# Where the output weights' split parts are kept, and who splits them: projections two and three in place of one and two

## The chip, the cores and the metric
The kernel runs on 1 core of a Trainium2 chip. The metric is the device time of one execution in microseconds (us). A core has five engines that run their own instruction streams in order and meet only by semaphores: TensorE (PE; its weight loads are PEld), VectorE (DVE), ScalarE (ACT), GpSimd (POOL) and SyncE (SP), which here only issues DMAs.

## The reference, cut
Inputs are four sequences of 512 rows and 512 channels. Computed is x plus attention of a modulated x, and then that plus a feed-forward of it:

```python
x = x + _L0_attn_ref(_L0_cond_ref(x, f, f, cond_w, cond_u, cond_512), Wq, Wk, Wv, Wo, betas)
x = x + _L0_ffn_ref(_L0_cond2_ref(x, f, f, cond2_w, cond2_u, cond_512), W1, W2, W3)
```

The attention has 16 heads of 128 and segments of 128 rows: in each segment a masked softmax attention and a recall from a memory that is updated by a delta rule, both joined, and the joined heads multiplied by the output weights:

```python
att = beta * att_mem + (1.0 - beta) * att_dot
out = att.reshape(Bsz, SEG, H * DV) @ Wo
```

The modulation is a decaying scan over the rows in both directions, a division and a sigmoid. The feed-forward has 2048 hidden channels, a gate and a Hadamard transform.

## The kernel before, in words
Every large product is made of three matmuls of float32r operands: a value is split into a high part (a copy rounded to fp32r) and a low part (value less high part), and the products high x high, high x low and low x high are summed (lines 489 to 491). So each weight tile must be split before use.

The attention is a loop over n = 0..31: two heads of one of the four sequences in each step, eight steps for a sequence. In step n TensorE also computes v, k and q for step n + 1, between the pieces of the attention of step n. After each four steps, at n = 4, 8, ..., 28, comes a burst: `wo(m, dc)` for dc = 0..3 multiplies what the last four steps have gathered in ah/al by the output weights. It takes eight tiles, the parts o (8m + 2 dc + half), two for each dc. The eighth projection stands behind the loop. All eight projections use the same eight tiles again, so part m % 8 names the weights.

`STREAM` is the order in which weight tiles are used, and each takes the next of six ring slots (wh, wl: high and low, 512 KB each). A tile comes into its slot in one of two ways:
- split: SP loads two halves of 256 KB from the input into the four buffers called stage; ScalarE writes the high part (`split_hi`, line 1247; for v of later steps and q GpSimd does it), then GpSimd the low part (`split_w`, line 1623), or VectorE (`low_o`, line 952) where `by_vector` says so;
- fetched again: where `again` says so, SP fetches both parts, 1 MB, from HBM (lines 1802, 1803), where they were stored after an earlier split (`keep`, lines 1814, 1815; two stores of 512 KB) if `kept` says so.

Before the change, o parts 0 to 7 (the first projection, at n = 4) are split, low parts 4 to 7 by VectorE; at n = 8 the parts 8 to 11 are fetched and 12 to 15 split by ScalarE and GpSimd. Parts 0 to 3 are kept at n = 4 and parts 12 to 15 at n = 8. All later ones are fetched. The v, k and q tiles are split and kept for n < 8 and fetched from n = 8 on.

SP has one queue. In it the calls `keep(upto)` and `load_w(upto)` alternate, with arguments that count from `here`, the place of v of n + 1 in STREAM. `keep` waits until a tile is split; a stage load waits until the low part two tiles before has been made (it frees the buffer); a fetch waits until the slot's last user is done. While SP waits, all behind it waits. The modulation's work is laid between the attention's pieces in slots k = 0..7 of step n (`behind(n, k)`) by a planner, `shared_out`, that hands out scan, reciprocal and other steps by cost against a room for each slot. ROOM is for ordinary steps, BURST_ROOM for bursts, and FIRST_BURST_ROOM for n = 4 only. They differ in slots 4 and 5:

```python
BURST_ROOM = (700, 900, 2200, 4500, 3600, 4800, 2900, 4400)
FIRST_BURST_ROOM = (700, 900, 2200, 4500, 2200, 600, 2900, 4400)
```

VectorE's order in the second half of a step is: `behind(n, 4)`, low_o of the first part, `recalled(n, 2)`, `sums`, `join(n, 0)`, `add_wo(., 1)`, low_o of the second, `behind(n, 5)`, `join(n, 1)`, low_o of the third and fourth, `add_wo(., 2)`, `add_wo(., 3)`. TensorE's in a burst: wo 0, transposes and update, wo 1, recall and P times V (line 643), wo 2, wo 3, update, then k and q of n + 1. Each half of wo waits for its part (`wait_split`).

Of the kernel before, what the change touches and what calls it, by code (L numbers as in the profile page):

```python
# [84 lines left out]
def is_burst(n):  # L85
    return n % 4 == 0 and n > 0
# [73 lines left out]
PLACE = {x: i for i, x in enumerate(STREAM)}  # L160
# [21 lines left out]
def kept(i):  # L182


    kind, m = STREAM[i]
    return kind in "vkq" and m < 8 or kind == "o" and (m < 4 or 12 <= m < 16)


def again(i):

    kind, m = STREAM[i]
    return kind in "vkq" and m >= 8 or kind == "o" and m >= 8 and not kept(i)


def by_scalar(i):
# [4 lines left out]
def by_vector(i):  # L200

    kind, m = STREAM[i]
    return kind == "o" and 4 <= m < 8


SPLIT = [i for i in range(NW) if not again(i)]
# [18 lines left out]
def adaln_attn_ffn(nc, xT_d, fT_d, cond_d, wu_d, wq_d, wk_d, wv_d, wo_d, betas_d,  # L225
# [9 lines left out]
    with ExitStack() as ctx:  # L235
# [170 lines left out]
        def halves(i, half):  # L406

            s = stage[(2 * SPLIT_NO[i] + half) % NSTAGE]
            hi, lo = ring(i)
            if STREAM[i][0] == "2":  # L410
                return (hi[:, :].rearrange("p (a n d) -> p n a d", a=2, n=8)[:, 4 * half:4 * half + 4],
                        lo[:, :].rearrange("p (a n d) -> p n a d", a=2, n=8)[:, 4 * half:4 * half + 4],
                        s[:, :].rearrange("p (n a d) -> p n a d", n=4, a=2))
            return hi[:, 512 * half:512 * half + 512], lo[:, 512 * half:512 * half + 512], s[:, :]
# [385 lines left out]
        def vector(e):  # L800
# [112 lines left out]
            def behind(n, k):  # L913
                for name, i, _ in STEPS[at[0]:UPTO[n, k]]:
                    if name[:2] == "lv":
                        level(i, int(name[2]))
                    elif name == "lo":
                        low_w2(i)
                    elif name in ("t0", "t1", "t2", "t3"):
                        z_times(i, int(name[1]))  # L920
                    elif name in ("nf", "nb", "df", "db", "mn", "mu", "ni", "n2", "di", "d2", "d3", "rc0", "rc1",
                                  "rc2", "rc3", "oy"):
                        scan(i, name)
                at[0] = UPTO[n, k]
# [21 lines left out]
            def low_o(m):  # L946

                i = PLACE["o", m]
                for half in range(2):
                    hi, lo, raw = halves(i, half)  # L950
                    w.wait_ge(a_wh, HI_A[i] + half + 1)
                    e.tensor_tensor(lo, raw, hi, ALU.subtract).then_inc(v_wl, 1)

            def maxima(n, j):
                w.wait_ge(d_mk, 16)
                w.wait_ge(d_b[0], 16)
                w.wait_ge(d_b[1], 16)
                w.wait_ge(pe_s, 2 * n + j + 1)
                w.wait_ge(pe_pt, 2 * (n - 1) + j + 1)
                w.wait_ge(a_p, 2 * (n - 1) + j + 1)  # L960
                for s in range(NSEG):
                    m = e.tensor_tensor_reduce(S[:, j, seg(s)], X[j][:, seg(s)], mask[:, :], 1.0, NEG, ALU.add,  # L962
                                               ALU.max, st[:, 0, j, s:s + 1])
                m.then_inc(v_mr, 1)
                w.wait_ge(v_mr, 2 * n + j + 1)
                e.tensor_scalar(st[:, 1, j, :], st[:, 0, j, :], -SCALE, None, ALU.mult).then_inc(v_mx, 1)
# [53 lines left out]
            def sigma(n, kind, j):  # L1020
                src, dst = (kT, sk) if kind == "k" else (qT, sq)
                w.wait_ge(a_kc if kind == "k" else a_qc, 2 * n + j + 1)
                w.wait_ge(a_ke if kind == "k" else a_qe, 2 * n + j + 1)
                if kind == "k":
                    w.wait_ge(pe_am, 6 * (n - 1) + 2 + j + 1)
                else:
                    w.wait_ge(pe_am, 6 * (n - 1) + 4 + j + 1)
                e.scalar_tensor_tensor(dst[:, j, :], src[:, j, :], 1.0, etmp[j][:, :], ALU.add,
                                       ALU.max).then_inc(v_sk if kind == "k" else v_sq, 1)
# [105 lines left out]
            for n in range(NN):  # L1135
                nx = n + 1
                more = nx < NN
                maxima(n, 0)
                maxima(n, 1)
                sigma(n, "q", 0)  # L1140
                behind(n, 0)
                if n > 0:
                    low_att(n - 1)
                sigma(n, "q", 1)
                behind(n, 1)
                memory(n, 0)
                if not more:
                    gate(0, 0, "1", G[0])
                behind(n, 2)
                recalled(n, 1)  # L1150
                if not more:
                    gate(0, 0, "3", G[1])
                behind(n, 3)
                memory(n, 1)
                if is_burst(n):
                    add_wo(n // 4 - 1, 0)
                behind(n, 4)
                if n == 4:
                    low_o(4)
                recalled(n, 2)  # L1160
                sums(n)
                join(n, 0)
                if is_burst(n):
                    add_wo(n // 4 - 1, 1)
                if n == 4:
                    low_o(5)
                if not more:
                    gate(0, 1, "1", G[0])
                if more and not is_burst(n):
                    sigma(nx, "k", 0)  # L1170
                behind(n, 5)
                join(n, 1)
                if n == 4:
                    low_o(6)
                    low_o(7)
                if is_burst(n):
                    add_wo(n // 4 - 1, 2)
                    add_wo(n // 4 - 1, 3)
                memory(n, 2)
                join(n, 2)  # L1180
                behind(n, 6)
                recalled(n, 3)
                join(n, 3)
                if is_burst(n):
                    sigma(nx, "k", 0)
                if more:
                    sigma(nx, "k", 1)
                else:
                    gate(0, 1, "3", G[1])
                behind(n, 7)  # L1190
# [572 lines left out]
        def sync(e):  # L1763
# [24 lines left out]
            def load_w(upto):  # L1788

                while load[0] < min(upto, NW):  # L1790
                    i = load[0]
                    load[0] += 1
                    if not again(i):
                        load_half(i, 0)
                        load_half(i, 1)
                        continue
                    kind, m = STREAM[i]
                    first = PLACE[kind, m % 8 + (8 if kind == "o" and m % 8 >= 4 else 0)]
                    w.wait_ge(d_keep[SLOT[first]], 32 * saves(SLOT[first], first + 1))
                    wait_used(w, BEFORE[i])  # L1800
                    hi, lo = ring(i)
                    e.dma_start(hi[:, :].bitcast(F32), high_s[kind][m % 8]).then_inc(d_back[SLOT[i]], 16)
                    e.dma_start(lo[:, :].bitcast(F32), low_s[kind][m % 8]).then_inc(d_back[SLOT[i]], 16)
# [63 lines left out]
            for n in range(NN):  # L1867
                nx, burst = n + 1, is_burst(n)
                more = nx < NN
                here = PLACE["v", nx] if more else PLACE["1", 0]  # L1870
                behind(n, 0)
                keep(here + 2)
                load_w(here + (6 if burst and n > 4 else 4))
                behind(n, 1)
                if n > 2 and is_burst(n - 2) and (n - 2) // 4 % 2 == 0:
                    fetch_x((n - 2) // 8)
                behind(n, 2)
                keep(here + 3)
                load_w(here + (8 if burst and n > 4 else 5))
                behind(n, 3)  # L1880
                if burst:
                    keep(here + 4)
                    load_w(here + (10 if n > 4 else 7))
                behind(n, 4)
                keep(here + (6 if burst else 4))
                load_w(here + (10 if burst else 6))
                behind(n, 5)
                if burst:
                    keep(here + 9)
                    load_w(here + 12)  # L1890
                behind(n, 6)
                if burst:
                    keep(here + 11)
                    load_w(here + 14)
                if more:
                    keep(here + (13 if burst else 5))
                    load_w(here + (15 if burst else 7))
                behind(n, 7)
# [104 lines left out]
```

## Time and profile before

| | us |
|---|---|
| median of 3 runs | 1669.19 |
| lowest and highest | 1668.13, 1670.24 |
| the profiled execution | 1668.93 |
| its span, first to last instruction | 1667.0 |
| TensorE busy | 1573.6 (94%) |
| VectorE busy | 1159.5 (70%) |
| ScalarE busy | 744.5 (45%) |
| GpSimd busy | 563.0 (34%) |
| moved by DMA | 264.39 MB |
| granted TensorE clock, mean | 0.989 |

The views are of the profiled execution; its times count from the first instruction, so 1.9 us of the 1668.93 lie around the span. An engine's idle time matters only where TensorE has to wait for it in the end. A granted clock of 1.00 is 2.4 GHz and 0.50 is 1.2 GHz.

### The profile page before, as it was taken

The page shows a single profiled execution, that of the slowest core. Times are in us where ns is not written, and L with a number is a line of the kernel's source. Part 1 is how long each engine was busy: PE and PEld are TensorE (multiplying, and loading weights), DVE is VectorE, ACT ScalarE, POOL GpSimd, SP SyncE. Part 2 cuts the span into 40 slices and gives each one's busy share as a digit, 9 for nine tenths or more (in the row PEclk, how much of TensorE's full clock was granted, in tenths as well). Part 3 has the DMA queues.
Part 4 walks back from the last instruction along what each step waited for, and adds up shares of the span by engine and source line. Part 5 has one row for each costly group of instructions (what it writes and reads, how often), then busy time and mean ns, then how long its engine had stood idle before and what let it go on. Part 6 is the DMA issues. An engine that isn't in the chain of part 4 may idle for free.

```text
span 1667.0 us, 26932 instructions
## 1 busy us (share of the span) xinstructions
PE 1573.6 (94%) x9696; PEld 1406.6 (84%) x9696; DVE 1159.5 (70%) x2688; ACT 744.5 (45%) x1623; POOL 563.0 (34%) x406
## 2 busy tenths in 40 slices
PE   0689979999999999999999999998999999999999
PEld 0579969898998999899999899888788888888887
DVE  8788959887888887887765763665787885333333
ACT  3366636535535534643554562652544442222221
POOL 4476555241232122121102100133655463343331
PEclk9799999999999999999999999999999999999999
DMA  3466566458365367456447646447211222221101
GB/s 135 153 212 209 189 239 236 174 185 334 136 228 196 125 230 253 146 187 224 162 157 283 233 179 240 142 153 252 90 57 51 65 68 105 98 64 39 51 14 51
DMA packets 111491, 264.39 MB, mean 159 GB/s; under 512 B 11088, under 2 KB 36096, under 8 KB 110464
## 3 DMA queue, kind: packets, MB, share of 16 engines
q1 hardware_dynamic: 92784, 235.41, 39.6%
q10 hardware_dynamic: 18576, 27.27, 5.3%
q8 instruction: 78, 1.28, 0.3%
q14 instruction: 53, 0.43, 0.1%
HBM read 214.38 MB, written 48.25 MB: 158 GB/s over the span
## 4 chain that ended last, share of the span: by engine, by line
PE 84%; DVE 8%; issue 3%; DMA 2%; ACT 1%; POOL 1%; ACTq 0%; SPq 0%; DVEq 0%; POOLq 0%
PE psG L489 15%; PE psG L491 15%; PE psG L490 15%; PE psX L489 3%; PE psX L643 3%; PE psX L490 3%; PE psX L491 3%; PE psX L598 3%; PE psZ L624 3%; PE psZ L615 2%; PE psZ L623 2%; PE psZ L490 2%; PE psZ L491 2%; PE psY L490 2%; PE psZ L489 2%
## 5 line engine op out<-in xcount | busy, mean ns | idle before, releaser
L1623 POOL TENSOR_TENSOR wl<-stage,wh 128x512 fp32r<-128x512 f32 x160 | 227.7, 1447 | 170.0 <-ACT wh L1247 168.7
L489 PE MATMUL psG<-yh,wh 128*128 128x512 f32 x632 | 258.2, 409 | 9.9 <-ACT etmp L1388 7.5
L491 PE MATMUL psG<-yh,wl 128*128 128x512 f32 x632 | 247.7, 392 | 0.0
L490 PE MATMUL psG<-yl,wh 128*128 128x512 f32 x632 | 247.4, 391 | 0.0
L1686 POOL TENSOR_TENSOR vs<-v,omb 128x512 f32<-128x512 f32 x64 | 95.9, 1519 | 340.7 <-PE psX L643 333.7
L1693 POOL TENSOR_TENSOR hl<-sg,hh 128x512 fp32r<-128x512 f32 x64 | 86.5, 1351 | 227.6 <-ACT hh L1462 227.5
L489 PE MATMUL psG<-ah,wh 128*128 128x256 f32 x512 | 146.7, 287 | 2.8 <-POOL wl L1623 1.7
L489 PE MATMUL psG<-wh,yh 128*128 128x256 f32 x496 | 146.8, 296 | 0.0
L489 PEld LDWEIGHTS psG<-yh,wh 128*128 128x128 f32 x632 | 119.9, 190 | 31.0 <-issue 8.1
L491 PE MATMUL psG<-ah,wl 128*128 128x256 f32 x512 | 144.9, 283 | 0.0
L490 PE MATMUL psG<-al,wh 128*128 128x256 f32 x512 | 144.8, 283 | 0.0
L491 PEld LDWEIGHTS psG<-yh,wl 128*128 128x128 f32 x632 | 119.2, 189 | 25.8
L491 PE MATMUL psG<-wh,yl 128*128 128x256 f32 x496 | 140.5, 283 | 0.0
L490 PE MATMUL psG<-wl,yh 128*128 128x256 f32 x496 | 140.4, 283 | 0.0
L490 PEld LDWEIGHTS psG<-yl,wh 128*128 128x128 f32 x632 | 120.0, 190 | 20.0
L1247 ACT ACTIVATE wh<-stage 128x512 fp32r<-128x512 f32 x154 | 89.1, 622 | 104.9 <-PE psZ L491 30.6
L1462 ACT ACTIVATE hh<-sg 128x512 fp32r<-128x512 f32 x64 | 40.5, 632 | 173.1 <-DVE sg L1048 173.1
L881 DVE RECIPROCAL DBK<-DF 128x128 f32<-128x128 f32 x120 | 107.8, 927 | 0.6
L1380 ACT ACTIVATE kT<-psG 128x512 f32<-128x512 f32 x62 | 37.0, 596 | 157.6 <-PE psG L491 157.6
L1413 ACT ACTIVATE S<-S,st 128x128 f32<-128x128 f32 x256 | 99.2, 389 | 17.1 <-issue 14.0
L489 PE MATMUL psX<-yh,wh 128*128 128x512 f32 x128 | 52.0, 407 | 56.4 <-POOL wl L1623 47.6
L962 DVE CUSTOM_DVE_ANT_0 S<-psX,mask 128x128 f32<-128x128 f32 x256 | 59.4, 286 | 65.7 <-PE psX L598 65.4
(197 smaller groups left out, 4267.6 us busy)
## 6 DMA issues: line engine op xcount, KB each, us to landing
wh<-high_o SPq DMA_DIRECT2D x52, 512.0 KB, 3.9
wl<-low_o SPq DMA_DIRECT2D x52, 512.0 KB, 5.2
stage<-in_w SPq DMA_DIRECT2D x64, 256.0 KB, 3.9
wh<-high_v SPq DMA_DIRECT2D x24, 512.0 KB, 4.0
wl<-low_v SPq DMA_DIRECT2D x24, 512.0 KB, 5.4
wh<-high_k SPq DMA_DIRECT2D x24, 512.0 KB, 4.2
wl<-low_k SPq DMA_DIRECT2D x24, 512.0 KB, 5.8
wh<-high_q SPq DMA_DIRECT2D x24, 512.0 KB, 4.5
```

What stands on the lines that cost most here:

```text
L489: e.matmul(out, lh, rh, start=first, stop=False, skip_group_check=check)
L490: e.matmul(out, lh, rl, start=False, stop=False, skip_group_check=check)
L491: return e.matmul(out, ll, rh, start=False, stop=last, skip_group_check=check)
L598: m = e.matmul(X[j][:, seg(s)], qT[:, j, seg(s)], kT[:, j, seg(s)], start=True, stop=True)
L624: e.matmul(Z[j][:, 129:258], sq[:, j, seg(s)], mem[:, j, 0:P + 1], start=True, stop=True).then_inc(pe_am, 1)
L881: e.reciprocal(dbk[:, 128 * j:128 * j + 128], df[:, 128 * j:128 * j + 128]).then_inc(v_rc, 1)
L962: m = e.tensor_tensor_reduce(S[:, j, seg(s)], X[j][:, seg(s)], mask[:, :], 1.0, NEG, ALU.add, ALU.max, st[:, 0, j, s:s + 1])
L1247: e.activation(hi, raw, ACT.Copy).then_inc(a_wh, 1)
L1413: m = e.activation(S[:, j, seg(s)], S[:, j, seg(s)], ACT.Exp, bias=st[:, 1, j, s:s + 1], scale=SCALE, accum_out=st[:, 2, j, s:s + 1])
L1623: e.tensor_tensor(lo, raw, hi, ALU.subtract).then_inc(p_wl, 1)
L1686: e.tensor_tensor(vs[:, :, j, :], v[n % 2][:, :, j, 0:P], omb[:, 128 * j:128 * j + 128].rearrange("p (a d) -> p a d", a=1).to_broadcast([P ...
L1693: e.tensor_tensor(hl[u % 2][:, j, :], hid(k)[:, :], hh[u % 2][:, j, :], ALU.subtract).then_inc(p_hl, 1)
```

## The change
The o parts kept are now 8 to 11 (at n = 8) and 20 to 23 (at n = 12), none at n = 4. Fetched are m >= 16 of parts 0 to 3 and m >= 24 of parts 4 to 7. So at n = 4 eight parts are split and none kept; at n = 8 eight parts are split, 12 to 15 with VectorE making the low parts, and 8 to 11 kept; at n = 12 parts 16 to 19 are fetched, and 20 to 23 split by ScalarE and GpSimd and kept. Over the kernel eight parts more are split and eight fewer fetched; eight are kept as before. SP's load arguments that held for n = 4 now hold for n = 8 too. The planner's rooms are left as they are.

```diff
     kind, m = STREAM[i]
-    return kind in "vkq" and m < 8 or kind == "o" and (m < 4 or 12 <= m < 16)
+    return kind in "vkq" and m < 8 or kind == "o" and (8 <= m < 12 or 20 <= m < 24)
...
-    return kind in "vkq" and m >= 8 or kind == "o" and m >= 8 and not kept(i)
+    return kind in "vkq" and m >= 8 or kind == "o" and m >= (16 if m % 8 < 4 else 24)
...
-    return kind == "o" and 4 <= m < 8
+    return kind == "o" and m < 16 and m % 8 >= 4
...
                 behind(n, 4)
-                if n == 4:
-                    low_o(4)
+                if n in (4, 8):
+                    low_o(2 * n - 4)
                 recalled(n, 2)
                 sums(n)
                 join(n, 0)
                 if is_burst(n):
                     add_wo(n // 4 - 1, 1)
-                if n == 4:
-                    low_o(5)
+                if n in (4, 8):
+                    low_o(2 * n - 3)
...
                 behind(n, 5)
                 join(n, 1)
-                if n == 4:
-                    low_o(6)
-                    low_o(7)
+                if n in (4, 8):
+                    low_o(2 * n - 2)
+                    low_o(2 * n - 1)
...
-                    first = PLACE[kind, m % 8 + (8 if kind == "o" and m % 8 >= 4 else 0)]
+                    first = PLACE[kind, m % 8 + ((8 if m % 8 < 4 else 16) if kind == "o" else 0)]
...
-                load_w(here + (6 if burst and n > 4 else 4))
+                load_w(here + (6 if burst and n > 8 else 4))
...
-                load_w(here + (8 if burst and n > 4 else 5))
+                load_w(here + (8 if burst and n > 8 else 5))
...
-                    load_w(here + (10 if n > 4 else 7))
+                    load_w(here + (10 if n > 8 else 7))
```

## Rows read from the trace of the kernel before

**Rows 1.** The page, part 1: busy us, share of the span, instructions.
```profile
PE 1573.6 (94%) x9696; PEld 1406.6 (84%) x9696; DVE 1159.5 (70%) x2688; ACT 744.5 (45%) x1623; POOL 563.0 (34%) x406
```

**Rows 2.** TensorE's waits, 100 to 420 us: total, times, longest.
```profile
PE psG L489 <- ACT etmp L1388: 7.5, 1, 7.5
PE psG L489 <- DMA wl<-low_q: 2.4, 1, 2.4
PE psG L489 <- POOL wl L1623: 1.7, 1, 1.7
PE psG L489 <- DVE wl L952: 1.0, 1, 1.0
```

**Rows 3.** The chain that ended last, n = 4: start, length, what.
```profile
221.45 3.01 DVE wl L952 x2
...
227.76 4.11 DMA stage<-in_wk
...
237.05 1.61 POOL wl L1623
...
239.57 5.75 DMA stage<-in_wk
...
247.75 0.77 PE psG L489
```

**Rows 4.** SP's queue in order of time, n = 4: start, length, what.
```profile
208.12 7.08 SPq L1786 DMA_DIRECT2D stage<-in_wo  x4
...
216.24 8.62 SPq L1786 DMA_DIRECT2D stage<-in_wo  x4
```

**Rows 5.** VectorE in order of time, n = 4: its subtractions of weights.
```profile
221.36 3.09 DVE L952 TENSOR_TENSOR wl<-stage,wh 128x512 fp32r<-128x512 f32 x2
...
226.41 2.48 DVE L952 TENSOR_TENSOR wl<-stage,wh 128x512 fp32r<-128x512 f32 x4
```

**Rows 6.** VectorE in order of time, n = 8: start, length, operation, [idle before].
```profile
343.99 1.22 DVE L835 TENSOR_TENSOR_SCAN DF<-dec,EK 128x512 f32<-128x512 f32 x1
...
356.12 1.76 DVE L881 RECIPROCAL DBK<-DF 128x128 f32<-128x128 f32 x2
358.72 0.17 DVE L984 RECIPROCAL rz<-psZ 128x2 f32<-128x2 f32 x1 [0.83 <-PE psZ L624]
...
361.22 0.41 DVE L1037 TENSOR_TENSOR xb<-xb,psG 128x256 f32<-128x256 f32 x1
361.55 1.76 DVE L881 RECIPROCAL DBK<-DF 128x128 f32<-128x128 f32 x2
...
364.19 2.12 DVE L835 TENSOR_TENSOR_SCAN DF<-dec,EK 128x512 f32<-128x512 f32 x1
...
368.41 0.58 DVE L1010 SCALAR_TENSOR_TENSOR pT<-psX,st,t 128x128 f32<-128x128 f32 x2
```

**Rows 7.** TensorE in order of time, n = 8: quarter's start, update behind, stalled q.
```profile
360.67 0.36 PE L489 MATMUL psG<-ah,wh 128*128 128x256 f32 x1
...
372.26 0.61 PE L615 MATMUL psZ<-delta,kn 128*128 128x129 f32 x4
...
381.18 0.50 PE L489 MATMUL psG<-yh,wh 128*128 128x512 f32 x1 [2.37 <-DMA wl<-low_q]
```

**Rows 8.** SP's queue in order of time, n = 8.
```profile
364.12 0.32 SPq L1830 DMA_DIRECT2D ratio_s<-OY  x1
...
371.95 1.13 SPq L1802 DMA_DIRECT2D wh<-high_q  x1
```

**Rows 9.** TensorE by microsecond: stretch, us, busy, granted clock, DMA share, GB/s.
```profile
244.00:245.00 1.00, 0.00 (x0) 0.60 0.92 238
...
251.00:252.00 1.00, 1.00 (x6) 0.99 1.07 369
```

**Rows 10.** Stretch: PE, PEld, DVE, ACT, POOL busy; granted clock, DMA share, GB/s.
```profile
225.00:235.00 10.00, 9.87 (x79) 9.57 (x78) 5.36 (x13) 3.40 (x6) 3.54 (x4) 1.00 0.50 159
```

**Rows 11.** SP's queue in order of time, n = 12.
```profile
489.99 0.32 SPq L1802 DMA_DIRECT2D wh<-high_q  x1
```

## The prediction, made before the changed kernel was run

> **What bounds the kernel now.** The page comes first: TensorE is busy 94% of the span [rows 1], so a change can win only where TensorE stands still, and loses wherever it makes TensorE wait. Second, who waited for whom on TensorE between 100 and 420 us, the stretch that holds the first two output projections (n = 4 and n = 8): it stood 7.5 us for ScalarE's etmp, 2.4 us for the low part of a q weight, 1.7 us and 1.0 us for the low parts of output weights [rows 2]. The 7.5 and the 1.7 and 1.0 lie at n = 4, the 2.4 at n = 8. So the two bursts hold 12.6 us that could be won. Third, the chain that ended last through the 7.5 us [rows 3]. Fourth, the queues in order of time on SP, VectorE and TensorE, for n = 4 [rows 4, 5] and n = 8 [rows 6 to 8].
>
> **n = 4, what the change takes away.** Four keeps go (parts 0 to 3: eight stores of 512 KB, 4.2 MB). SP passes straight on to its stage loads: the loads that start at 208.12 no longer stand behind the keep of part 2, and those at 216.24 no longer behind the keep of part 3 [rows 4], a gain of 1 to 3 us for when parts 4 and 6 land. Is that on the path? The chain says no [rows 3]. What ends the 7.5 us is: VectorE splits part 5 (221.45), later parts 6 and 7; that frees the stage into which k of n = 5 is loaded (227.76, 4.1 us to land); GpSimd splits k and then q (until 238.7); SP, which keeps q first, then loads k of n = 6 (239.57, 5.75 us to land); ScalarE, which has that split ahead of etmp in its order, gets there at 247. VectorE's start on part 5 follows its join(n, 0), which waits for TensorE's own P times V, not for a part 4 or 5 that came late. All keeps left in that chain are those of k, q and v, and they stay. The stores of part 3, issued by 216, are over long before 227: from 225 to 235 the DMA engines are busy 0.50 [rows 10]. So I price the removal at nothing, cover being this chain. Bounds: a gain of all of it, 7.5 us of standing plus what the clock gives back (below), if the landings of 4.1 and 5.75 us are short of bandwidth because of older stores; and nothing on the other side, since no wait is added at n = 4.
>
> A page of the Trainium skill, "DMA: Bandwidth & Descriptors" (section "Where 436 GB/s comes from"), puts the ceiling of a core's ports at about 435 GB/s; by it the 4.2 MB are an estimated 9.6 us of transfer, and if the burst were bound by transfer the change would win about that. The share of 0.50 ahead of the chain's first landing speaks against it here.
>
> **n = 8, first what goes.** Parts 8 to 11 are no longer fetched (4 x 1 MB) but loaded (4 x 0.5 MB) and split; the same number of keeps stands there, but of parts 8 to 11, which come before and early in the burst as those of parts 0 to 3 did at n = 4. Now the keeps of 12 to 15 are held up by the store of OY to ratio_s at 364.12, go out in a bunch, and push the fetch of q to 371.95 [rows 8]; it lands late and TensorE stands 2.37 us at 381.18 [rows 7]. Afterwards no keep follows that store, q is fetched right behind it, around 368 to 369, and TensorE asks for it later. I take the whole 2.4 us as won.
>
> **n = 8, what comes.** VectorE gets the low parts of 12 to 15: eight subtractions. Four in a row took 2.48, so 0.62 each, but the two of part 5, beside GpSimd's multiplication of V, took 3.09 together [rows 5]. Where they stand in VectorE's order matters more than their 5 us: parts 14 and 15 stand behind behind(8, 5) and join(8, 1). At n = 4 the plan leaves only a short step there (FIRST_BURST_ROOM has 600 in place of 4800), and this plan is not changed for n = 8. So at n = 8 two reciprocals, OY and two scans stand ahead of part 14. Working it out in before's times:
> 1. VectorE ends its two reciprocals at 357.88 and has 0.83 us free before the recall [rows 6]. Part 12 takes 1.24, ends 359.1: everything up to the add at 361.22 comes 0.4 later.
> 2. GpSimd now splits parts 10 and 11 from 345 to 354, beside VectorE's scans, which slows both: a scan took 2.12 beside GpSimd and 1.22 without it [rows 6]. Bounds 0 to 1.1 us; I take 0.35. So part 13 starts at 361.55 + 0.75 = 362.3.
> 3. Part 13 is, as part 5 was, beside the multiplication of V: 3.09, ends 365.4 (bounds 1.24 and 3.09).
> 4. Two reciprocals and OY: 364.19 - 361.55 = 2.64, to 368.0 [rows 6].
> 5. Two scans: 368.41 - 364.19 = 4.2 us before, with GpSimd splitting beside them [rows 6]. That splitting is gone, so I take twice 1.15 (1.22 less the overlap of neighbours), 2.3, to 370.3; bounds 2.3 and 4.2.
> 6. join(8, 1) 0.5, then part 14, 1.24: 372.0.
>
> TensorE: the third quarter of the projection starts at 360.67, and two quarters end at 372.26, so a quarter is 5.8 and a part 2.9 [rows 7]. It wants part 13 at 363.57 and gets it at 365.4: 1.85 us. It would start the last quarter at 360.67 + 5.8 + 1.85 = 368.3 and gets part 14 at 372.0: 3.7 us. Part 15 is ready 1.24 later, in time. Sum 5.55. Behind the stall stand the k and q projections of n = 9 on TensorE; VectorE waits for them, so it recovers there, and its order behind part 15 was idle for 3 us before.
>
> ScalarE's eight copies and GpSimd's four pairs for 8 to 11 come as at n = 4, ahead of need; but two are close. Part 11 is due about 355 (ahead of 360.67 by a part, 2.9, and the recall and P times V), and ScalarE takes it after an exponential that waits for VectorE until about 350, so GpSimd ends it near 354. And ScalarE copies part 12 before it copies pT, which TensorE needs for P times V near 359, and part 12 lands, as part 4 did, some 5 us after its load was issued, near 356. Both priced at 0, bound 1 us each.
>
> **n = 12.** It becomes the old n = 8: four fetched, four split by ScalarE and GpSimd and kept. There the keeps cost 2.37 us through the store to ratio_s. At n = 12 the tiles are of the first modulation, whose OY isn't stored, so nothing bunches them. The fetch of q, at 489.99 now [rows 11], would wait until part 23 is kept, about 498, and is wanted at 510. Priced at 0, bound 2.4.
>
> **Sum.** -2.4 + 5.55 = +3.2 on a profiled execution of 1668.93 us (span 1667.0), which is 0.26 below the median of the three, 1669.19 (1668.13 to 1670.24). 1669.19 + 3.2 = 1672.4; from the profiled one 1672.1. Between them I say 1672.3.
> Bounds of this case: step 3 at its low end and step 2 at 0 give part 14 at 369.9, a stall of 3.4, and +1.0: 1670. Every step at its upper end: part 14 at about 375.5, a stall of 9, and +6.7: 1676.
>
> **Rivals.**
> 1. The forecast, VectorE late with 13 and 14, clock kept: 1672.3. Chance 0.34.
> 2. The same with the clock lost. At n = 4 TensorE stood until 247.75 for 7.5 us [rows 2, 3], from 240.2, and in the microsecond from 244 the granted clock was 0.60, on its way from 2.4 to 1.2 GHz; it was back only from 251 (0.99), though work began at 247.75 [rows 9]. So about 3.3 us of work went at half speed: 1.6 us more. A stall of 3.7 us, with one of 1.85 three us before it, comes near the four microseconds after which it fell there. 1672.3 + 1.7 = 1674.0. Chance 0.22. (The Trainium skill, "TensorE: Matmul & The Clock Gate", section "What's actually happening", has a throttled default that activity releases; the rows above agree.)
> 3. The other side: the old stores do hold up the landings at n = 4, and the 7.5 us go with 1.6 of clock. Against it: the chain [rows 3] and the 0.50 [rows 10]. For it: 5.75 us to land where others took less. 1672.3 - 9.1 = 1663.2, less where only part of it goes. Chance 0.12.
> 4. VectorE's new work finds room (the steps ahead of part 14 run faster, or part 13 does), and the q stall goes: between -2.4 and +0.5, about 1667.3. Against it: VectorE's order there [rows 6], which leaves no gap of this size between 361.2 and 368.4. Chance 0.16.
> 5. More is late: part 11 or pT, scans slowed after all, or the 2.4 us return at n = 12. From one of these at full size, with the clock: 1677. Chance 0.16.
>
> **How the numbers follow.** A measurement can tell about 0.2%, 3.3 us, from no change: 1665.9 and 1672.5 are the borders. Faster: rival 3 and a little of 4, 0.14. The same: most of 4 (0.14) and two thirds of 1 (0.22), 0.36. Slower: the rest of 1 (0.12), 2 and 5, 0.50. The range leaves out rival 3 and the tail of 5: 1666 to 1677. The case of my forecast alone spans 1670 to 1676.
>
> **What would show it.** In the profile after: TensorE waits for VectorE's wl at n = 8 in two places, 1 to 2 us and 3 to 4 us; scans of VectorE stand between its first and second pair of subtractions there; no wait for low_q; the 7.5 us for etmp at n = 4 unchanged within 1 us; no new wait at n = 12; GpSimd's wl count up from 160 to 168, VectorE's from 8 to 16, ScalarE's wh by 16; 4.2 MB less moved. The prediction is wrong if the etmp wait shrinks, or if VectorE's part 14 is done by 368.

## The result
The changed kernel takes 1675.74 us (median of 6 runs, 1673.14 to 1678.43), the kernel before 1669.53 beside it (6 runs, 1668.13 to 1670.45). The ratio is 1.0038, 95% interval 1.0025 to 1.0051: 6.3 us slower, 4.2 to 8.5. Run again beside two of the experiments it was 1677.16 against 1671.70, ratio 1.0032, 1.0021 to 1.0042. The forecast was 1672.3 with a range of 1666 to 1677, and slower by over 0.2% had a chance of 0.50. The profiled execution took 1675.9, its span is 1673.9 against 1667.0.

The page after, to set beside [rows 1], and the line of the bytes moved:

```profile
PE 1578.8 (94%) x9696; PEld 1411.1 (84%) x9696; DVE 1169.0 (70%) x2696; ACT 754.0 (45%) x1639; POOL 572.8 (34%) x414
...
DMA packets 111492, 260.21 MB, mean 155 GB/s; under 512 B 11088, under 2 KB 36096, under 8 KB 110464
```

Counts and bytes are as announced: 8 instructions more on VectorE and GpSimd each, 16 on ScalarE, 4.2 MB less moved. TensorE does the same 9696 matmuls and is busy 5 us longer, in part since some of them ran at the lower clock (below).

TensorE's waits after, from 100 to 420 us, to set beside [rows 2] (waiting instruction, what it waited for: total, times, longest):

```profile
PE psG L489 <- ACT etmp L1388: 6.3, 1, 6.3
PE psG L489 <- DVE wl L952: 5.7, 3, 3.5
PE psG L489 <- POOL wl L1623: 1.9, 2, 1.7
```

and from 420 to 700 us, where the kernel before had no wait for a weight:

```profile
PE psG L489 <- DMA wl<-low_q: 2.0, 1, 2.0
```

Three things are to be seen: etmp's wait at n = 4 is 1.2 us shorter, VectorE's low parts cost 4.7 us more, and the wait for low_q has moved from the first to the second stretch.

To see where the 6.9 us of span came from I took the last step of each quarter of a projection, VectorE's add into xb (line 1037), as a mark. From the two traces in order of time:

| stretch | before | after | difference |
|---|---|---|---|
| start to first add at n = 4 | 211.87 | 212.89 | +1.02 |
| n = 4, first to last add | 21.99 | 22.00 | 0.01 |
| to the first add at n = 8 | 118.87 | 118.51 | -0.36 |
| n = 8, first to last add | 19.73 | 26.39 | +6.66 |
| to the first add at n = 12 | 112.00 | 109.11 | -2.89 |
| n = 12, first to last add | 19.73 | 19.74 | +0.01 |
| to the first add at n = 16 | 109.52 | 110.86 | +1.34 |
| to the last add of the last projection | 534.54 | 534.39 | -0.15 |
| to the end of the span | 518.75 | 520.01 | +1.26 |

The first and the last line are not the change's: in the profiles of all kernels of this study the first add lies between 210.9 and 212.9, and the last stretch between 517.3 and 520.4, with no order in them; the changed kernel itself, run again, has 517.75 us in the last stretch where it had 520.01. What lies between sums to +4.6 (+4.8 in the changed kernel run again).

VectorE after, in order of time, through n = 8, to set beside [rows 6]:

```profile
357.68 1.76 DVE L881 RECIPROCAL DBK<-DF 128x128 f32<-128x128 f32 x2
359.36 1.92 DVE L952 TENSOR_TENSOR wl<-stage,wh 128x512 fp32r<-128x512 f32 x2
...
363.26 0.41 DVE L1037 TENSOR_TENSOR xb<-xb,psG 128x256 f32<-128x256 f32 x1
363.59 2.16 DVE L952 TENSOR_TENSOR wl<-stage,wh 128x512 fp32r<-128x512 f32 x2
365.67 1.75 DVE L881 RECIPROCAL DBK<-DF 128x128 f32<-128x128 f32 x2
367.46 0.75 DVE L886 SCALAR_TENSOR_TENSOR OY<-NF,tf,DBK 128x512 f32<-128x512 f32 x1
368.32 1.22 DVE L835 TENSOR_TENSOR_SCAN DF<-dec,EK 128x512 f32<-128x512 f32 x1
369.46 1.20 DVE L838 TENSOR_TENSOR_SCAN NF<-dec,EKV 128x512 f32<-128x512 f32 x1
370.57 0.58 DVE L1010 SCALAR_TENSOR_TENSOR pT<-psX,st,t 128x128 f32<-128x128 f32 x2
371.07 2.49 DVE L952 TENSOR_TENSOR wl<-stage,wh 128x512 fp32r<-128x512 f32 x4
```

The two scans stand ahead of parts 14 and 15 (the last row, four subtractions), and VectorE has no gap. TensorE in order of time, to set beside [rows 7]:

```profile
361.62 0.36 PE L489 MATMUL psG<-ah,wh 128*128 128x256 f32 x1
...
365.90 0.36 PE L489 MATMUL psG<-ah,wh 128*128 128x256 f32 x1 [1.16 <-DVE wl L952]
...
372.51 0.55 PE L489 MATMUL psG<-ah,wh 128*128 128x256 f32 x1 [3.50 <-DVE wl L952]
```

It waits 1.16 us for part 13 and 3.50 for part 14. And TensorE by microsecond (stretch, us, busy, granted clock, DMA share, GB/s):

```profile
371.00:372.00 1.00, 0.00 (x0) 0.98 1.00 281
372.00:373.00 1.00, 0.49 (x2) 0.50 0.71 229
...
375.00:376.00 1.00, 1.00 (x9) 0.81 1.05 428
```

The clock fell to 1.2 GHz at the end of the 3.5 us, just before part 14 was ready, and was back within 375: 2.9 us of work at half speed, 1.4 us lost. Of the 6.66 us at n = 8 the two waits are 4.7, the clock 1.4, and 0.2 is a wait for GpSimd's part 11; 0.4 is not assigned.

### The profile page after: what moved, and what is told of

Its sections match the earlier page's. It is cut to its first block, busy times and chain, and to the rows that moved or that the text cites. A ratio compares the mean times of both kernels' runs of the same rounds, so it can differ in the third digit from the quotient of the medians.

```text
span 1673.9 us, 27003 instructions
## 1 busy us (share of the span) xinstructions
PE 1578.8 (94%) x9696; PEld 1411.1 (84%) x9696; DVE 1169.0 (70%) x2696; ACT 754.0 (45%) x1639; POOL 572.8 (34%) x414
## 4 chain that ended last, share of the span: by engine, by line
PE 83%; DVE 9%; issue 3%; DMA 2%; ACT 1%; POOL 1%; ACTq 0%; SPq 0%; DVEq 0%; POOLq 0%
PE psG L489 15%; PE psG L491 15%; PE psG L490 15%; PE psX L489 3%; PE psX L490 3%; PE psX L491 3%; PE psX L643 3%; PE psX L598 3%; PE psZ L624 2%; PE psZ L615 2%; PE psZ L623 2%; PE psY L490 2%; PE psY L489 2%; PE psZ L490 2%; PE psZ L491 2%
## 5 line engine op out<-in xcount | busy, mean ns | idle before, releaser
L1623 POOL TENSOR_TENSOR wl<-stage,wh 128x512 fp32r<-128x512 f32 x168 | 242.1, 1466 | 184.5 <-ACT wh L1247 183.2
L1247 ACT ACTIVATE wh<-stage 128x512 fp32r<-128x512 f32 x170 | 98.8, 622 | 114.3 <-PE psZ L491 31.4
L489 PEld LDWEIGHTS psG<-ah,wh 128*128 128x128 f32 x512 | 98.7, 193 | 8.8 <-issue 7.4
```

The source lines that it names most:

```text
L489: e.matmul(out, lh, rh, start=first, stop=False, skip_group_check=check)
L1247: e.activation(hi, raw, ACT.Copy).then_inc(a_wh, 1)
L1623: e.tensor_tensor(lo, raw, hi, ALU.subtract).then_inc(p_wl, 1)
```

## The experiments
All ratios are against the kernel before on the same chip, with 95% intervals. The kernel before had medians of 1669.5 to 1672.2 in the comparisons, as much as most effects here, so I go by the ratio and by the stretches between adds.

### VectorE's help alone
On the kernel before, with `low_o` of 2n - 4 to 2n - 1 called at n = 8 too:
```diff
-    return kind == "o" and 4 <= m < 8
+    return kind == "o" and m < 16 and m % 8 >= 4
...
-                if n == 4:
+                if n in (4, 8):
...
```

> The kernel before with the other part of the change alone: VectorE makes the low parts of 12 to 15 at n = 8 in place of GpSimd; every keep and fetch lies as before. Theory (VectorE's order is what costs): TensorE waits for VectorE's wl at n = 8, 4 to 6 us in all, with a clock fall of 1 to 2 us more; the keeps of 14 and 15 come later and push the fetch of q, so its wait stays. Time 4 to 8 us over before, as much as the whole change or more. Rival (GpSimd's extra four parts are what made the difference): within 2 us of before.

1675.23 us, ratio 1.0022 (1.0012 to 1.0032), 3.7 us slower (2.0 to 5.4); the profiled execution has a span of 1673.9, as the whole change. TensorE's waits from 340 to 400 us, first of this kernel:

```profile
PE psG L489 <- DVE wl L952: 4.5, 2, 3.5
PE psG L489 <- DMA wl<-low_q: 1.2, 1, 1.2
```

and of the changed kernel:

```profile
PE psG L489 <- DVE wl L952: 4.7, 2, 3.5
PE psG L489 <- POOL wl L1623: 0.2, 1, 0.2
```

The same 3.5 us. From first to last add at n = 8 it takes 27.3 us. So VectorE's part alone makes a loss of this size; by the ratio its middle is a little under the 4 to 8 that I gave it. The clock cost more here than in the changed kernel: it was back only in 378, so work from 372.30 on lost some 3 us, against 1.4.

### The keeps moved, without VectorE
On the changed kernel, with the condition put back in all three places:
```diff
-    return kind == "o" and m < 16 and m % 8 >= 4
+    return kind == "o" and 4 <= m < 8
...
-                if n in (4, 8):
+                if n == 4:
...
```

> The changed kernel with the low parts of 12 to 15 left to GpSimd, as before the change; the keeps lie as in the changed kernel. Theory: TensorE has no wait for VectorE's wl at n = 8, at most 2 us for GpSimd's; no q wait at n = 8 (saved 2.4), a q wait of about 2 us at n = 12: in all 1668 to 1671, the same as before. Rival (moving the keeps is itself what costs): 1674 or more though VectorE splits nothing at n = 8.

1669.55 us, ratio 0.9992 (0.9981 to 1.0004): no difference from before. At n = 8 there are 21.2 us from first to last add, 1.4 over before, of which 1.1 are waits for GpSimd's wl; the wait for low_q is 2.1 us and lies at n = 12. The rival, that moving the keeps is what costs, falls.

### One half of the keeps, without VectorE
On the kernel before:
```diff
-    return kind in "vkq" and m < 8 or kind == "o" and (m < 4 or 12 <= m < 16)
+    return kind in "vkq" and m < 8 or kind == "o" and (m < 4 or 20 <= m < 24)
...
-    return kind in "vkq" and m >= 8 or kind == "o" and m >= 8 and not kept(i)
+    return kind in "vkq" and m >= 8 or kind == "o" and (8 <= m < 12 or m >= 16) and not kept(i)
```

> The kernel before with one half of the change, without VectorE's help: parts 0 to 3 are kept at n = 4 as before; the keeps of the other half move from 12 to 15 (n = 8) to 20 to 23 (n = 12), split by GpSimd. Theory (the four keeps and the split carry their own q stall with them): the wait for low_q at n = 8 goes, one of about 2 us comes at n = 12, time as before within 2 us. Rival (n = 12 has room, as I forecast): no q wait at all and 2 to 3 us faster.

1668.77 us, ratio 0.9988 (0.9977 to 0.9999). Its only wait for low_q is 1.8 us, at n = 12; the stretch from n = 8 to 12 is 109.1 (2.9 shorter), that from 12 to 16 110.9 (1.4 longer). The stall goes where the keeps go. This is the place where the rival was my own forecast, that n = 12 has room, and by the wait it fell. The time is less clear: 2.0 us faster by the ratio (0.2 to 3.8) lies on the border between the two expectations, and in the profile the stall costs 1.4 us at n = 12 where it had cost 2.9 at n = 8.

### No stores at n = 4
The kernel before without the keeps of parts 0 to 3. It leaves out their stores and later fetches v tiles of the same size in their place, so it computes the projections from the second on with wrong weights and serves for timing alone:
```diff
-    return kind in "vkq" and m < 8 or kind == "o" and (m < 4 or 12 <= m < 16)
+    return kind in "vkq" and m < 8 or kind == "o" and 12 <= m < 16
...
+                    if kind == "o" and m % 8 < 4:
+                        kind = "v"
...
```

> The kernel before without the keeps of parts 0 to 3 (eight stores of 512 KB at n = 4), and later fetches of those parts read the kept v tiles of the same size in their place, so the projections from the second on are computed with wrong weights; all else is equal. Theory (the chain of splits sets the 7.5 us at n = 4, the stores do not): etmp's wait stays between 6 and 8 us, time 1668 to 1670.5. Rival (the stores hold up the landings): the wait falls by 3 us or more and time to 1666 or less.

1671.16 us, ratio 1.0009 (0.9999 to 1.0019). etmp's wait is 6.3 us, as in the changed kernel, 7.5 before. The stretch from the last add at n = 4 to the first at n = 8 is 118.2. Over the profiles it lies between 118.2 and 119.2 in the three kernels that store at n = 4 and keep SP's order there (mean 118.7), and between 117.1 and 118.5 in the seven that don't store (mean 118.0). So the four keeps at n = 4 are worth some 0.7 us in that stretch, from ranges that overlap, and rival 3, which gave them 7.5 us and the clock, falls. The total is no evidence here, since this kernel's q stall at n = 8 was longer: 4.0 us and a clock fall, 3.9 us more than before in the stretch to n = 12. SP's queue and TensorE there:

```profile
368.25 0.70 SPq L1804 DMA_DIRECT2D wh<-high_q  x1
```
```profile
381.68 0.80 PE L489 MATMUL psG<-yh,wh 128*128 128x512 f32 x1 [4.01 <-DMA wl<-low_q]
```

Here q's fetch was issued 3.7 us earlier than in the kernel before (371.95, [rows 8]), and TensorE waited 1.6 us longer for it. The time of issue alone doesn't set this stall.

### SP's order at n = 4
On the kernel before:
```diff
+                if n == 4:
+                    load_w(here + 13)
                 if burst:
                     keep(here + 11)
                     load_w(here + 14)
```

> The kernel before with one change in SP's order at n = 4: the stage loads of k of n = 6 go ahead of the keeps of k and q of n = 5. Theory (those loads stand behind the keep of q and land behind its 1 MB): they are issued at about 236 and 238.5 in place of 239.6, land by 242, etmp's wait falls from 7.5 to 3 to 5 us, and time by 3 to 5 us, to about 1665. Rival (ScalarE's or GpSimd's own work is next late, or the keeps only trade places): under 1 us gained.

1666.41 us, ratio 0.9975 (0.9963 to 0.9988), 4.2 us faster. etmp's wait is 3.4 us. SP's queue and ScalarE in this kernel, in order of time:

```profile
235.03 3.05 SPq L1786 DMA_DIRECT2D stage<-in_wk  x2
238.12 0.43 SPq L1814 DMA_DIRECT2D high_k<-wh  x1
```
```profile
237.62 0.64 ACT L1247 ACTIVATE wh<-stage 128x512 fp32r<-128x512 f32 x1 [1.26 <-DMA stage<-in_wk]
240.90 0.63 ACT L1247 ACTIVATE wh<-stage 128x512 fp32r<-128x512 f32 x1 [2.64 <-DMA stage<-in_wk]
```

Both halves of k are there by 240.9, where the chain of [rows 3] had them at 245.3. That the chain runs through the keep of q, as the prediction read it, is shown. The loads also landed faster: ScalarE had the first half 2.6 us after its issue (235.03 to 237.62), where behind the keep of q it took 5.75 us to land [rows 3].

### SP's order at n = 4 and n = 8
The edit above, and on the kernel before:
```diff
+                if n == 8:
+                    load_w(here + 11)
                 if burst:
                     keep(here + 9)
                     load_w(here + 12)
```

> The kernel before with two changes in SP's order: at n = 4 k of n = 6 is loaded ahead of the keeps of k and q of n = 5, and at n = 8 q of n = 9 is fetched ahead of the keeps of parts 13 to 15. Theory: the gain of the first alone (4 to 5 us) plus the q wait at n = 8 (2.2 us): 6 to 7 us faster than before. Rival (the keeps are pushed onto v, k, q of the next steps and stall there): no more than the first alone.

1660.83 us, ratio 0.9948 (0.9936 to 0.9961): 8.7 us faster, the best kernel of the study. No wait for low_q is left, etmp's is 3.3 us. Between first add and last it takes 929.05 us, 7.3 less than before, a little over the 6 to 7 expected; the rest of the span's 8.3 is in the two outer stretches that vary anyway.

### The changed keeps with that order
On the changed kernel: GpSimd in place of VectorE, `load_w(here + 13)` ahead at n = 4 and `load_w(here + 11)` ahead at n = 12.

> The changed keeps and splits, with GpSimd in place of VectorE for 12 to 15, and SP's order altered as in the fastest kernel so far: at n = 4 k of n = 6 is loaded ahead of the keeps of k and q, at n = 12 q of n = 13 is fetched ahead of the keeps of 21 to 23. Theory (what the change moves is worth nothing by itself once the q stall is gone at either place): no wait for low_q, etmp's wait 2 to 4 us, time within 3 us of that fastest kernel, 0.993 to 0.996 of before. Rival (having no stores at n = 4 is worth something with the loads ahead): 2 us or more under it.

1663.79 us, ratio 0.9953 (0.9941 to 0.9965), no wait for low_q, etmp's 2.9. The stretch from n = 12 to 16 is 109.53 us, as long as before (109.52), where the kernel with the keeps moved, which differs there in SP's order alone, has 111.18: the order of q's fetch and the keeps makes the stall at n = 12. The intervals of this and the last kernel overlap, from two comparisons. By the stretches splitting 8 to 11 in place of fetching them costs 1.3 us at n = 8 (21.0 us from first to last add, of which 1.0 are waits for GpSimd's wl), and elsewhere I see no worth in where the keeps lie once SP's order is mended.

### The plan's rooms
On the changed kernel:
```diff
+SECOND_BURST_ROOM = (700, 900, 2200, 4500, 2200, 600, 2900, 10000)
...
-        left = min(left, 0) + (FIRST_BURST_ROOM if n == 4 else BURST_ROOM if is_burst(n) else ROOM)[k]
+        left = min(left, 0) + (FIRST_BURST_ROOM if n == 4 else SECOND_BURST_ROOM if n == 8 else BURST_ROOM if is_burst(n) else ROOM)[k]
```

> The changed kernel with the planner's rooms at n = 8 cut in slots 4 and 5 as at n = 4 (2200 and 600 in place of 3600 and 4800), the steps taken out laid into slot 7 (10000 in place of 4400), so that the plan is the same again at n = 9. Theory (VectorE's order sets the loss at n = 8): the wait for part 14 (3.5 us before a clock fall) is gone or under 0.7 us, the clock stays up at n = 8, part 13 may still cost 1 to 2 us, and time falls by 3.5 to 6 us against the changed kernel, to about 1670 to 1672. Rival (GpSimd's and ScalarE's extra splitting sets the loss, or the moved steps come late elsewhere): time stays within 1.5 us of the changed kernel's 1675.7, with waits of the same sum in n = 8 or n = 9.

1678.27 us, ratio 1.0054 (1.0036 to 1.0072). The stall for part 14 went: 21.2 us from first to last add at n = 8. But the rival had it right: TensorE stood again, 5.8 us, at the scores of n = 9. TensorE's wait from 370 to 400, and ScalarE in order of time:

```profile
PE psX L599 <- issue: 5.8, 1, 5.8
```
```profile
390.41 0.72 ACT L1260 ACTIVATE EU<-EU,wu 128x512 f32<-128x512 f32 x1 [3.35 <-DVE EU L823]
391.04 0.58 ACT L1381 ACTIVATE qT<-psG 128x512 f32<-128x512 f32 x1
```

The trace gives no releaser for that wait, but the copy of q to qT, which the scores need, stands in ScalarE's order behind two exponentials that wait for VectorE's moved steps, and the scores start at 391.72. The reading is from order and times; the next run bears it out.

The same with 4400 in slot 7 and the 5600 spread over n = 9, 700 in each slot:

> The changed kernel with the rooms at n = 8 cut in slots 4 and 5 as at n = 4, and the 5600 taken out spread over the eight slots of n = 9, 700 each (the earlier try had them all in slot 7 of n = 8, where ScalarE waited for VectorE ahead of the copy of q and TensorE stood 5.8 us). Theory: the waits for parts 13 and 14 stay as small as in that try (about 1 us), the 5.8 us at the scores of n = 9 go, and time is 1669 to 1672 against 1675.7 of the changed kernel. Rival (VectorE is full around n = 9 wherever the steps lie): a wait of 3 us or more appears in n = 9 or 10.

1671.60 us, ratio 1.0001 (0.9992 to 1.0011). The 5.8 us are gone, VectorE's wl cost 2.0 us over n = 4 and n = 8 together, and q at n = 12 3.0.

### VectorE's order
The changed kernel once more, and then with `low_o(2 * n - 2)` and `low_o(2 * n - 1)` of n = 8 ahead of `behind(n, 5)` and `join(n, 1)`:
```diff
+                if n == 8:
+                    low_o(2 * n - 2)
+                    low_o(2 * n - 1)
                 behind(n, 5)
                 join(n, 1)
-                if n in (4, 8):
+                if n == 4:
```

> The changed kernel once more, on the same chip as the next two, for comparison: 3 to 8 us over before; waits for VectorE's wl at n = 8 of 1.2 and 3.5 us, for low_q at n = 12 of 1 to 3 us.

> The changed kernel with one thing altered: at n = 8 VectorE makes the low parts 14 and 15 ahead of behind(8, 5) and join(8, 1), not behind them. Plan, keeps and fetches stay. Theory (the place in VectorE's order costs, not its amount of work): from the first to the last add of the projection at n = 8 some 21.5 us in place of 26.4, the wait for part 14 under 0.5 us, no fall of the clock there, time 4 to 6 us under the changed kernel and so within 2 us of before. Rival (VectorE has too much to do around n = 8 wherever it stands): the stall reappears behind the burst, and less than 2 us is gained.

1677.16 (1.0032, 1.0021 to 1.0042) against 1670.17 (0.9999, 0.9989 to 1.0010): the same work in another order is 5.5 us faster by the ratios. The changed kernel run again has the waits expected: 1.16 and 3.50 us for VectorE's wl at n = 8 and 2.3 for low_q at n = 12. VectorE in the kernel with its order altered, in order of time:

```profile
361.63 3.32 DVE L952 TENSOR_TENSOR wl<-stage,wh 128x512 fp32r<-128x512 f32 x4
366.52 1.29 DVE L952 TENSOR_TENSOR wl<-stage,wh 128x512 fp32r<-128x512 f32 x2 [1.56 <-ACT wh L1250]
```

Part 14 is done at 364.95, TensorE doesn't wait for it, and part 15 waits only for its high part. The wait for part 13 is still 1.16 us. The stretch at n = 8 is 22.4 us (26.4 in the changed kernel, run again), 0.9 over the 21.5 expected, part of it since the last two adds now wait for VectorE. No stall came back behind the burst.

## Why the prediction was right, and where it was off
**n = 4, the stores priced at nothing.** Held in the main, not to the letter. From the last add there to the next burst it is -0.36 us in the pair of profiles, 0.7 in the mean of ten. But the prediction called itself wrong if etmp's wait shrank, with a margin of 1 us, and it shrank by 1.2 (7.5 to 6.3), by 1.6 in the changed kernel run again (5.9). The kernels with the stores at n = 4 and SP's old order have 6.1 to 7.6 us, the seven without the stores 5.5 to 6.3, so a small part of the wait did stand on the stores. Most of the 1.2 was lost again in the clock. It came back at 251 before [rows 9], but only within 252 in the changed kernel:

```profile
251.00:252.00 1.00, 1.00 (x4) 0.50 1.07 332
252.00:253.00 1.00, 1.00 (x5) 0.75 0.93 281
```

So 5.0 us of work from 247.53 on went at half speed where 3.3 had, 0.9 us more lost. The rest of rival 3 is answered by two runs: without the stores nothing like 7.5 us is gained, with the loads ahead of the keeps 4.2 us are. By the Trainium skill's ceiling of about 435 GB/s in "DMA: Bandwidth & Descriptors" ("Where 436 GB/s comes from") the same 4.2 MB would have been an estimated 9.6 us. No gain of that size shows here, since the chain waits on an order and not on those bytes.

**n = 8, VectorE late.** Held in its order and nearly in its sum. Counted from the first add at n = 8, which came 0.67 later than before, part 14 was done at 371.07 + 1.24 - 0.67 = 371.6 in before's times; the sum had 372.0. The terms inside were off and nearly cancelled. VectorE ended its reciprocals 0.9 us later rather than 0.35, most of it in one step that took 1.51 us beside GpSimd's EKV where it had taken 0.41:

```profile
356.13 1.51 DVE L877 TENSOR_SCALAR DF<-DF 128x512 f32<-128x512 f32 x1
```

Part 12 took 1.92 beside another multiplication, 0.7 over its 1.24; the steps up to the add gave 0.4 back, and part 13 started at 362.9 in place of 362.3. It took 2.16, not 3.09. The two scans took 2.25, as forecast (2.3); but GpSimd's splitting had stood beside the first of them only, until 365.2, and two other multiplications of GpSimd beside the rest. The two stalls were 1.16 and 3.50 where 1.85 and 3.7 were forecast, 4.7 in place of 5.55. That the place of parts 14 and 15 in VectorE's order is the cause of the second is shown by two kernels that leave its work as it is and change its order or its plan.

**The clock.** The case with it had 0.22, that without it 0.34; it came, 1.4 us where I had put 1.7. At n = 8 it fell in all three profiles that have the wait of 3.50 us, and cost 1.4, 1.5 and, with VectorE's help alone, some 3 us. At n = 4 it went either way. TensorE's clock in the kernel with SP's order mended there, after a wait of 3.4 us for etmp:

```profile
242.00:243.00 1.00, 0.35 (x2) 0.99 1.02 418
243.00:244.00 1.00, 1.00 (x4) 0.50 1.04 426
```

and in the one with both orders mended, after 3.3 us:

```profile
243.00:244.00 1.00, 0.00 (x0) 1.00 1.04 426
244.00:245.00 1.00, 0.89 (x4) 1.00 1.00 410
```

The one fell to 1.2 GHz, the other did not. No run here shows what decides between them, so that the size of 1.7 was nearly met is in part luck.

**The q stall at n = 8.** Held: -2.89 in its stretch, 2.4 forecast; q's fetch was issued at 368.66, 368.0 in before's times, where 368 to 369 was forecast.

**n = 12 priced at nothing.** This step failed. The forecast looked only at the store to ratio_s, which bunches the keeps at n = 8, and put the fetch of q at 498 in before's times. It was issued then: 502.38, and this burst lay 4.44 later. But SP in order of time shows what stands ahead of it:

```profile
495.37 0.42 SPq L1802 DMA_DIRECT2D wh<-high_k  x1
...
496.31 0.43 SPq L1814 DMA_DIRECT2D high_o<-wh  x1
...
501.50 0.84 SPq L1815 DMA_DIRECT2D low_o<-wl  x1
502.38 0.80 SPq L1802 DMA_DIRECT2D wh<-high_q  x1
```

The keeps of all four parts are bunched here too, behind the stage loads, the last of which waits for part 21 (done at 494.9) and was issued by 495.3. TensorE wants q at 514.98 and gets it only at 516.95, 13.7 us after the issue of its low part at 503.23. I had counted when the fetch is issued, and not what the engines had still to move: from 500 to 525 they were busy 0.99 to 1.03 in each stretch of 5 us, at 398 to 415 GB/s. What was issued before q is not the whole of it. By the GB/s of those stretches I estimate that the 6.6 MB issued from 495 up to and with q would have been moved by about 513, in time; but 8.0 MB were moved from 495 to 517, so the fetches of v and k issued behind it, at 505 and 508, took a share. That is argued from these numbers; that SP's order makes the stall is shown by the run with q's fetch ahead of the keeps. The term is +1.34 in place of 0.

**Sum.** Forecast -2.4 + 5.55 = +3.2. Measured between the marks: -0.36 + 6.66 - 2.89 + 1.34 - 0.13 = +4.6, and 6.3 (4.2 to 8.5) by the runs, 5.4 (3.5 to 7.0) the second time. In the pair of profiles the other 2.3 us of the span lie in the two stretches that vary from profile to profile; why the medians differ by more than 4.6 is not settled. What came is not the case called most likely, with its clock kept (1672.3, chance 0.34), but rival 2 together with the stall at n = 12 that rival 5 names (0.16). The clock and n = 12 are missing from the forecast of 1672.3, which is 3.4 us low; the range held because it had room for both. One bound was added up wrongly: with every step at its upper end part 14 comes at 372.0 + 0.75 + 1.9 = 374.7, not 375.5, and the case ends at 1675, not 1676. Nothing hangs on it.

## What to carry to other kernels
Work given to an engine that has time on average must be looked up in that engine's order: here 5 us of subtractions cost TensorE 4.7 us of waiting and 1.4 us of clock, mostly because reciprocals and scans stood ahead of the last of them. Once these stood ahead of the scans, the stretch was 4 us shorter and the total no longer differed from before. Before moving a store that seems to be in the way, find the wait that stands on it; here the loads wanted to go ahead of the stores in one queue (8.7 us), and which burst the stores lie in was worth some 2 us at most. A stall that hangs on a bunch of transfers goes with the bunch: price the new place by all the bytes that have to move before the wanted one is needed, those issued shortly behind it too, and not by the time at which it is issued.

## What was not expected of the hardware
With the DMA engines busy all the time, 1 MB fetched took 13.7 us from the issue of its second half to TensorE's start at n = 12, and 12.7 us at n = 8 in the kernel without stores at n = 4, while the median for the low parts of o is 5.2 us from issue to landing. Small steps of VectorE were slowed by GpSimd as well as large ones: 1.51 us in place of 0.41 for the one on line 877. And without the stores at n = 4, the last half of part 7 was there later, not sooner: ScalarE got it at 229.55 in the changed kernel, where before it came at 227.02, with the first add only 1.02 later. I have no cause for that; it cost nothing there.
